# Second layer of a two-layer graph network on one Trainium2 core: table products of 26 candidates with the penalty rows inside them, and twelve of 40 edge columns by TensorE in place of ten

## The reference: what is computed

```python
x = _layernorm(x + _L0_gnn_ref(x, src, dst, edge_attr_3, edge_attr_10, edge_weight, W1, W2))
x = _layernorm(x + _L1_gnn_ref(x, attn_w, src, dst))
...
def _L1_gnn_ref(h, attn_w, src, dst):
    s_src = h @ attn_w[:d]
    s_dst = h @ attn_w[d:]
    e = s_src[src] + s_dst[dst]
    e = jnp.where(e >= 0, e, LEAKY_SLOPE * e)
    m = jax.ops.segment_max(e, dst, num_segments=N)
    ex = jnp.exp(e - m[dst])
    denom = jax.ops.segment_sum(ex, dst, num_segments=N)
    alpha = ex / denom[dst]
    return jax.ops.segment_sum(h[src] * alpha[:, None], dst, num_segments=N)
```

## Time and profile before

| | |
|---|---|
| time, median of 3 runs | 5710.63 us (5705.38 to 5717.29) |
| span of the profiled execution | 4918.3 us |
| time of a run beside that span | 792.3 us |
| TensorE busy (matmul) | 3925.7 us, 80% of the span |
| GpSimd busy | 3457.8 us, 70% |
| VectorE busy | 3366.4 us, 68% |
| ScalarE busy | 1665.0 us, 34% |

### The profile page before, as it was taken

How to read it: one execution, slowest core, us unless ns; L and a number is a source line. 1 busy time by engine, 2 the same in 40 slices (tenths; PEclk the granted TensorE clock), 3 DMA queues, 4 the chain that set the end, 5 groups by cost and what they waited for, 6 DMA issues and landing times. The chain is left out here.

```text
span 4918.3 us, 76839 instructions
## 1 busy us (share of the span) xinstructions
PE 3925.7 (80%) x22447; PEld 2433.8 (49%) x22447; DVE 3366.4 (68%) x5756; ACT 1665.0 (34%) x3062; POOL 3457.8 (70%) x3515
## 2 busy tenths in 40 slices
PE   0007999999999999999999600899999999999950
PEld 0004555545544555555555300677777777777740
DVE  4517999999999999999999540455555555555532
ACT  3005666666665666666666300001010100001000
POOL 5777777777666666666663177677777777777766
PEclk9999999999999999999999855899999999999975
DMA  9412222222222222222221000222222222222211
GB/s 327 135 35 50 46 44 45 44 44 46 47 44 43 43 43 43 43 43 43 49 46 30 21 11 14 55 48 46 45 48 48 45 47 49 49 49 49 49 27 25
DMA packets 266830, 253.17 MB, mean 51 GB/s; under 512 B 182298, under 2 KB 237026, under 8 KB 263867
## 3 DMA queue, kind: packets, MB, share of 16 engines
q1 hardware_dynamic: 157118, 174.83, 13.1%
q0 software_dynamic: 109024, 72.30, 9.5%
q10 hardware_dynamic: 462, 4.00, 0.3%
HBM read 160.55 MB, written 90.34 MB: 51 GB/s over the span
## 5 line engine op out<-in xcount | busy, mean ns | idle before, releaser
L626 POOL DMA_INDIRECT edge<-xp_d,idx x1440 | 1437.2, 998 | 634.6 <-issue 358.5
L1231 POOL DMA_INDIRECT gxb<-tab_d,idxb x1200 | 1290.6, 1075 | 376.6 <-issue 324.9
L890 DVE TENSOR_TENSOR prod<-G_ps,hid 128x1000 f32<-128x1000 f32 x1200 | 1385.5, 1192 | 67.0 <-ACT hid L685 39.1
L782 PE MATMUL G_ps<-FT,wst 64*128 64x500 f32 x4800 | 937.9, 434 | 38.2 <-DVE prod L890 38.2
L1266 PE MATMUL G_ps<-tb,hot 125*126 125x500 f32 (+1 forms) x3200 | 675.5, 364 | 333.0 <-DVE hotk L1288 299.7
L792 PE MATMUL R_ps<-prod,red 128*32 128x500 f32 x4800 | 769.4, 601 | 0.0
L1266 PEld LDWEIGHTS G_ps<-tb,hot 125*126 125x126 f32 x3200 | 546.3, 192 | 449.1 <-issue 349.8
L782 PEld LDWEIGHTS G_ps<-FT,wst 64*128 64x128 f32 x4800 | 421.6, 187 | 467.1 <-issue 263.9
L766 PE MATMUL T_ps<-ident,HL 125*128 125x125 f32 x3200 | 519.0, 285 | 129.1 <-DVE HL L880 128.4
L679 ACT ACTIVATE FT<-T_ps 128x500 fp32r<-128x500 f32 x800 | 470.0, 590 | 204.5 <-PE T_ps L766 192.6
L766 PEld LDWEIGHTS T_ps<-ident,HL 125*128 125x128 f32 x3200 | 332.7, 141 | 411.6 <-issue 274.4
(11 more groups left out here) (247 smaller groups left out, 4636.9 us busy)
## 6 DMA issues: line engine op xcount, KB each, us to landing
xd_d<-zeros SPq DMA_DIRECT2D x16, 1562.5 KB, 29.0
y_d<-zrb SPq DMA_DIRECT2D x40, 595.0 KB
edge<-xp_d,idx POOLq DMA_INDIRECT x1440
xv<-xd_d SPq DMA_DIRECT2D x40, 560.0 KB
y_d<-zr SPq DMA_DIRECT2D x40, 560.0 KB
edge<-sel_d SPq DMA_DIRECT2D x40, 546.9 KB
gxb<-tab_d,idxb POOLq DMA_INDIRECT x1200
em<-in_edge_attr SPq DMA_DIRECT2D x40, 175.0 KB
```

The source lines that it names most:

```text
L626: nc.gpsimd.indirect_dma_start(out=edge_c[:, i, 8:8 + DIM], out_offset=None, in_=xp_d, in_offset=bass.IndirectOffsetOnAxis(col, 0)).then_i ...
L782: last = Tn.matmul(G_ps[(k * 3 + i) % 2][:, a * 512:a * 512 + GW], wst[a * 64:(a + 1) * 64, (2 * i + l) * 128:(2 * i + l + 1) * 128], FT[k ...
L890: V.tensor_tensor(prod[k][i][:, :].rearrange("p (a e) -> p a e", a=2), gv, hid[k][:, :].rearrange("p (a e) -> p a e", a=1).broadcast_to([1 ...
L1231: nc.gpsimd.indirect_dma_start(out=gx[h][:, c * T1:(c + 1) * T1], out_offset=None, in_=tab_d, in_offset=bass.IndirectOffsetOnAxis(idx[h][: ...
```

## The change

A group of candidates is 26 wide in place of 25 (`KL`), so 104 nodes stand on a partition and 121 partitions hold them all; seven partitions of 128 are free. These take the penalty: `tb[0]` holds on them -2^100 for each candidate whose place is not the partition's (the 4 x 7 free rows hold at least 26 places), and the node rows of SP hold there the place of each edge within its group (`sel_d[1]`) where the other 121 hold its partition and group. The column vectors `iot` are shifted on these seven partitions to match. So the same four one-hots per chunk, now on 128 partitions, select the data and the penalty, and `far`, `hotk` and their two products per column go. The features are split 17 and 16 (442 and 416 wide). `XC` is 12, so GpSimd gathers 28 columns per chunk. The table is no longer made piece by piece from `x1e`: its layout of 104 nodes per partition is read back from `tab_d` into `xt1` by three DMAs of SP, and ScalarE and VectorE make the high and low parts from that, four copies and four subtractions after the fourth piece. The first block makes two more index patterns and the shifted `iot`.

```diff
-    XC = 10
+    XC = 12
...
-    KL = 25
+    KL = 26
+    PR = 121
+    NR = NG4 * KL
+    KR = PG - PR
...
-    FU = 20
-    GS = KL * (DIM + 1) + 1
+    FU = 17
+    GS = KL * (DIM + 1)
...
+                    nc.gpsimd.iota(own_i[:, :], [[0, 1]], base=0, channel_multiplier=1).then_inc(S("a_iota"), 1)
+                    nc.gpsimd.iota(kio_i[:, :], [[1, KL]], base=0, channel_multiplier=0).then_inc(S("a_iota"), 1)
...
+                    step(V.tensor_scalar(krow[:, :], krow[:, :], float(PR) - 0.5, -float(PR), ALU.is_ge, ALU.mult))
+                    for g in range(NG4):
+                        step(V.scalar_tensor_tensor(iot[:, g:g + 1], krow[:, :], g + 1.0, iot[:, g:g + 1], ALU.mult, ALU.add))
...
                     step(V.memset(sd[:, :], 0.0))
-                    for l in range(2):
-                        step(V.memset(tb[l][:, :].rearrange("p (g w) -> p g w", w=GS)[:, :, GS - 1].bitcast(f32), 0.0))
-                    step(V.tensor_scalar(far[:, :].rearrange("p (f k) -> p f k", k=KL),
-                                         ident[0:KL, 0:KL].rearrange("p (f k) -> p f k", f=1).broadcast_to([KL, FU, KL]), -1.0, FAR, ALU.add, ALU.mult))
...
+                    V.memset(xt1[:, :], 0.0).then_inc(S("c_tb0"), 1)
+                    V.memset(tb[1][:, :].bitcast(f32), 0.0).then_inc(S("c_tb0"), 1)
+                    for g in range(NG4):
+                        V.tensor_scalar(by_feature(tb[0], g, PG), kio[:, :].rearrange("p (f k) -> p f k", f=1).broadcast_to([PG, DIM + 1, KL]),
+                                        iot[:, g:g + 1], -FAR, ALU.not_equal, ALU.mult).then_inc(S("c_tb0"), 1)
...
+                    act.wait_ge(S("c_tb0"), 2 + NG4)
+                    act.wait_ge(S("c_tab"), 80)
+                    for g in range(NG4):
+                        nc.scalar.activation(by_feature(tb[0], g, PR), by_node(g), ACT.Copy).then_inc(S("c_hi"), 1)
...
+                    sp.wait_ge(S("c_tb0"), 1)
+                    rows = tab_d[0:(PR - 1) * NR, :].rearrange("(p k) f -> p (k f)", k=NR)
+                    for r in (slice(0, PS), slice(PS, PR - 1)):
+                        sp.dma_start(xt1[r, :], rows[r]).then_inc(S("c_tab"), 16)
...
                         for l in range(2):
                             for g in range(NG4):
                                 for (f0, f1, w), ps in zip(FUS, slot):
-                                    nc.tensor.matmul(ps[0:PE2, 0:w], hot[h][:, g * XP + j * P:g * XP + j * P + PE2],
-                                                     tb[l][:, g * GS + f0 * KL:g * GS + f0 * KL + w], start=(l == 0 and g == 0), stop=False)
-                        for (f0, f1, w), ps in zip(FUS, slot):
-                            last = nc.tensor.matmul(ps[0:PE2, 0:w], hotk[h][:, j * P:j * P + PE2], far[:, 0:w], start=False, stop=True)
+                                    last = nc.tensor.matmul(ps[0:PE2, 0:w], hot[h][:, g * XP + j * P:g * XP + j * P + PE2],
+                                                            tb[l][:, g * GS + f0 * KL:g * GS + f0 * KL + w],
+                                                            start=(l == 0 and g == 0), stop=(l == 1 and g == NG4 - 1))
...
-                        V.tensor_scalar(hotk[h][:, 0:XP], nodek[h], iot[0:KL, 0:1], None, ALU.is_equal).then_inc(S("d_hot"), 1)
```

More of the change, by code:

```diff
@@ L55, in gnn_resnorm_kernel @@
     C121 = 1.5 ** 0.5
-    XC = 10
+    XC = 12
     CG = C - XC
     NG4 = 4
-    KL = 25
+    KL = 26
+    PR = 121
+    NR = NG4 * KL
+    KR = PG - PR
+    assert PR * NR >= N and (PR - 1) * NR < N and NG4 * KR >= KL
     XP = XC * P
-    FU = 20
-    GS = KL * (DIM + 1) + 1
+    FU = 17
+    GS = KL * (DIM + 1)
     PE2 = P + 1
@@ L190, in gnn_resnorm_kernel @@
             SELB = NSEL // 4
-            iot_i = sbt("iot_i", [P, NG4], i32)
+            iot_i = sbt("iot_i", [PG, NG4], i32)
+            own_i = sbt("own_i", [PG, 1], i32)
+            krow = sbt("krow", [PG, 1])
+            kio_i = sbt("kio_i", [PG, KL], i32)
             ssel, psel, ksel, gsel = [sq[:, a * NSEL:(a + 1) * NSEL] for a in range(4)]
@@ L1029, in gnn_resnorm_kernel @@
         both = ExitStack()
-        tb = [both.enter_context(nc.sbuf_tensor(f"tb{l}", [P, NG4 * GS], f32r)) for l in range(2)]
-        far = both.enter_context(nc.sbuf_tensor("far", [KL, FU * KL], f32r))
-        assert NG4 * KL == NP and KP == KL and NPIECE == NG4
+        tb = [both.enter_context(nc.sbuf_tensor(f"tb{l}", [PG, NG4 * GS], f32r)) for l in range(2)]
         with ExitStack() as st:
@@ L1043, in gnn_resnorm_kernel, with by_feature, by_node @@
             sd = sbt("sd", [PG, NP])
-            def by_feature(ap, i):
-                return ap[:, i * GS:i * GS + KL * (DIM + 1)].rearrange("p (f k) -> p f k", k=KL)
-            def by_node(i):
-                return piece_of(x1e, i, DIM + 1).rearrange("p k f -> p f k")
+            xt1 = sbt("xt1", [PR, NR * (DIM + 1)])
+            def by_feature(ap, g, rows):
+                return ap[0:rows, g * GS:(g + 1) * GS].rearrange("p (f k) -> p f k", k=KL)
+            def by_node(g):
+                return xt1[:, g * GS:(g + 1) * GS].rearrange("p (k f) -> p f k", f=DIM + 1)
             with nc.Block() as block:
@@ L1123, in _ @@
                         nc.scalar.activation(stt[:, 2 * NP + i * KP:2 * NP + (i + 1) * KP], stt[:, NP + i * KP:NP + (i + 1) * KP], ACT.Sqrt).then_inc(S("ln_std"), 1)
-                        act.wait_ge(S("c_x1e"), i + 1)
-                        nc.scalar.activation(by_feature(tb[0], i), by_node(i), ACT.Copy).then_inc(S("c_hi"), 1)
+                    act.wait_ge(S("c_tb0"), 2 + NG4)
+                    act.wait_ge(S("c_tab"), 80)
+                    for g in range(NG4):
+                        nc.scalar.activation(by_feature(tb[0], g, PR), by_node(g), ACT.Copy).then_inc(S("c_hi"), 1)
                 @block.sync
@@ L1148, in gnn_resnorm_kernel @@
             gx = [sbt(f"gxb_{h}", [PG, C * T1]) for h in range(2)]
-            hot = [sbt(f"hot_{h}", [P, NG4 * XP + 2], f32r) for h in range(2)]
-            hotk = [sbt(f"hotk_{h}", [KL, XP + 2], f32r) for h in range(2)]
-            nodes = [edge[0:P, h * XP:(h + 1) * XP] for h in range(2)]
-            nodek = [edge[0:KL, (2 + h) * XP:(3 + h) * XP] for h in range(2)]
-            FUS = ((0, FU, FU * KL), (FU, T1, (T1 - FU) * KL + 1))
+            hot = [sbt(f"hot_{h}", [PG, NG4 * XP + 2], f32r) for h in range(2)]
+            nodes = [edge[:, h * XP:(h + 1) * XP] for h in range(2)]
+            FUS = ((0, FU, FU * KL), (FU, T1, (T1 - FU) * KL))
             SLOTS = [(G_ps[0][:, 0:512], G_ps[0][:, 512:1024]), (G_ps[1][:, 0:512], G_ps[1][:, 512:1024]),
@@ L1179, in load_nodes @@
                         if not isinstance(ch, int):
-                            sp.wait_ge(S("d_hot"), ch * 5 - 5)
+                            sp.wait_ge(S("d_hot"), ch * NG4 - NG4)
                             sp.sem_inc(S("go"), 1)
-                        for a, t in ((0, nodes[h]), (1, nodek[h])):
-                            rows = sel_d[a].rearrange("i p -> (i p)")[bass.ds(ch * XP, XP)].rearrange("(a f) -> a f", a=1).broadcast_to([t.shape[0], XP])
-                            if a == 0:
-                                by_rows(sp, t, rows, S(f"d_nd{h}"))
-                            else:
-                                sp.dma_start(t, rows).then_inc(S(f"d_nd{h}"), 16)
+                        for a, r0, r1 in ((0, 0, PS), (0, PS, PR), (1, PR, PG)):
+                            rows = sel_d[a].rearrange("i p -> (i p)")[bass.ds(ch * XP, XP)].rearrange("(a f) -> a f", a=1).broadcast_to([r1 - r0, XP])
+                            sp.dma_start(nodes[h][r0:r1, :], rows).then_inc(S(f"d_nd{h}"), 16)
                     def load(ch, h, t):
```

32 lines of the change are left out of this document (17 added, 15 removed).

## The result

The changed kernel took 5749.99 us (median of 4, 5737.16 to 5756.64), the kernel before 5708.01 beside it (5697.20 to 5717.29): ratio 1.0071, 95% interval 1.0055 to 1.0087. The forecast was 5693 us, 0.3% faster, with a range of 5650 to 5722; the kernel is 0.7% slower, outside the range.

The account below looks back on a forecast made before the run. Gathers were taken to bound the second layer's loop at 41.4 us per chunk, the new bound being 40.9. Loop -22.4 and +4.6 between the layers made -17.8 us, from 5710.6 to 5693 us; range 5650 to 5722.

Parts of the forecast that it names:

- 792.3 us beside the span: Whole run: time of 5710.6 us less the profiled span of 4918.3, left unchanged in the sum.
- Period 40.9 us: Second layer's loop, per chunk: 39.8 us plus 1.1 for slow columns, in place of 41.4; loop 22.4 us shorter.
- 14.7 us and eight columns: Second layer's chunk: VectorE's absence of 14.7 us plus eight columns of 3.14 gives 39.8 us, above the gathers' 39.0.
- Column of 3.14 us: TensorE, second layer's loop: eight new pairs of 0.392 us with no pauses left, 3.14 us a column.
- rivals 2 and 3: Second-layer columns: 2, border pause stays, 3.34 us, 5714 us (0.20); 3, all pauses stay, 3.56 us, 5785 us (0.11).
- rival 4: TensorE streams at the full rate, column 2.86 us, gathers bind at 39.0 us: 5617 us (chance 0.04).
- Stall of 2.1 us: TensorE, once per chunk: VectorE's absence of 14.7 us less the 12.6 us covered by four columns.
- 0.72 x 1.5: TensorE after the stall: 13 in 18 chance of a slow column costing 1.5 us, 1.1 us per chunk.
- Rival 1: TensorE's clock stays up, no slow columns, period 39.8 us: 5651 us (chance 0.17).
- The gathers' 39.0 us: GpSimd, second layer's loop: 28 gathers of 1.25 us plus 4.0 per chunk, under the 39.8 us bound.
- +4.6 between the layers: VectorE's clears and fills ahead of the carried row add 4.6 us to the path, bounds +2 and +8.
- Hidden work: Table through DRAM, preparing work before the first layer, and larger node rows: all covered, costing nothing.

Follow-up runs that it names:

- experiment 1: Both kernels rerun unchanged: the kernel before 5713.35 us, ratio 0.9996, span 5711.1; the changed kernel 5753.44 us, ratio 1.0085.
- new_table_10: Changed kernel with ten columns by TensorE in place of twelve, the new table alone: 5713.39 us, ratio 1.0002 to the kernel before.
- base_again: The kernel before, run again unchanged for a second trace: 5713.35 us, ratio 0.9996.
- experiment 3: Changed kernel with the next one-hot made after four picks: 5729.79 us with twelve columns, 5704.91 us with ten.
- experiment 7: Changed kernel making only 4 of a chunk's 28 gathers after the first two chunks, leaving work out: 5624.51 us, ratio 0.9695 to the kernel before.
- Experiment 4: Changed kernel with six fills of the new table moved below the addition of the carried row: 5742.62 us, ratio 1.0068 to the kernel before.
- experiment 5: Changed kernel without the waits that pace GpSimd's gathers by TensorE's columns: 6451.49 us, ratio 1.1311 to the kernel before.
- narrow_products: Changed kernel with 14 of a column's 16 products streaming only 128 columns, leaving work out: 5771.57 us, ratio 1.0110 to the kernel before.
- few_gathers: Changed kernel making only 4 of a chunk's 28 gathers after the first two chunks: 5624.51 us, ratio 0.9695 to the kernel before.
- after_third: Changed kernel run once more unchanged, beside the best version: 5756.54 us, ratio 1.0094 to the kernel before.

## Why the prediction was wrong, point by point

- **The step that failed** is in the sum: "The time of a run holds 792.3 us beside the span (5710.6 less 4918.3), which I leave as it is". They lie inside the span, 627 and 138 of them in the two loops (experiment 1). The section ahead of the prediction made the same step, where it says that they lie outside what the trace shows. I had taken a trace that was 14% shorter than the time for the shape of the run and the missing time for a constant. With it fell **"Period 40.9 us"**: the executions that are timed have a pause of 4.0 us per chunk in the changed kernel.
- *Why the pause turns a gain into a loss.* Before, the gathers bind; TensorE has slack, its pause goes into that, and only GpSimd's waits in it, 3.5 us per chunk in new_table_10 and 4.1 in base_again, add to its gathers' 41 to 41.5 (44.9 measured, mean over 39 periods). After, TensorE and VectorE bind, as forecast, and 4.0 us stand in their cycle with no slack beside them. It is not a fixed cost on top: experiment 3 took 3.9 us out of the same cycle and the pause grew by 3.8. The forecast's period of 14.7 us and eight columns is a cycle with no slack left. The new bound itself was forecast, and without the pause it measures what was forecast (41.06 in experiment 7 against 40.9); what it was exposed to was not.
- *Column of 3.14 us*: right (3.135), and nothing at the border, so rivals 2 and 3 fall, though the time came out on rival 3's side. The excess over full rate stayed, so rival 4 falls. By the Trainium skill's rule on the issue gap, as cited in the prediction, it would be 2.90; the trace decides against it for this pair. That section gives the rule for an isolated product and says that at large widths it over-counts a stream of products with their weight loads; here the stream takes 392 ns per pair and the rule gives 362, so it under-counts.
- *Stall of 2.1 us and "0.72 x 1.5" for the slow column*: 2.49 and 1.43 (33 of 38 chunks were slow, 13 in 18 assumed). Together 0.7 us per chunk too little, 27 us over the loop: by itself this would have made 5693 into 5720, just inside the range. Rival 1, the clock that stays up, falls.
- *The gathers' 39.0 us below the bound, and no wait of VectorE for them*: right. GpSimd stands, as forecast, but for 3.4 us ahead of a chunk's first gather in place of 1 to 2, and 3.0 more in the pause (means, each beyond the usual 0.30).
- *+4.6 between the layers*: 7.7, inside its bounds (+2 and +8). The clears came as forecast (2.92 us each), but the four fills take 4.02 us in place of the 2.16 that the one-hots' rate gave, and 1.4 us of idle time stand ahead of the two clears. GpSimd's first DMA, which the upper bound would have held up, comes 17.5 us after the last edge product, as before (17.6). Experiment 4 shows that the 7.7 were avoidable.
- *Hidden work*: no sign of a cost. From the stored row between the layers to the first table product are 295.3 us in the changed kernel and 298.8 in the kernel before, so the table's way through DRAM is covered; the first edge product starts at 415.6 to 424.8 us in the traces with the new preparing block and at 416.3 in the second trace of the kernel before.

What stays open: why gathers beside TensorE's products slow the latter down and delay their counts. Whether it is their packets, their instructions or something else of theirs was not taken apart. Half the bytes gathered and 96 more instructions on ScalarE left it as it was; the clock and the load of the DMA engines do not explain it (1.00 and 0.08 in the pause shown above). Nothing points to a refill of TensorE's instructions either: from 3925 to 5500 us, 34 chunks with their pauses, the DMA queues of the changed kernel are these two (packets, MB, share of 16 engines), and no instruction queue is among them:

```profile
q1 hardware_dynamic: 27000, 52.03, 11.0%
q0 software_dynamic: 30976, 16.42, 8.2%
```

(The Trainium skill, "Runtime: NRT & Kernel Launch", section "Instruction fetch mechanics", has a sequencer refill its instructions in blocks by a DMA queue of its own, and stall where a branch leaves its window. By it the pause could have been such a refill; the rows show none.) Open too is why the first execution had no pauses, and the 627 us in the first layer's loop, on which nothing was tried.

## What to carry to other kernels

Compare a trace's span with the run's time before anything is taken from it; where they differ by more than runs do, the trace isn't of the run, and a balance of engines worked out from it says nothing of slack. Moving work from the engine that binds to one that is nearly as full exposes every pause that slack had swallowed. And when a split between two engines changes, the waits that pace one by the other belong to the change: here `c % 3`, right for 30 gathers to ten columns, was left standing for 28 to twelve.

## What the runs showed of the hardware that I had not expected

- With GpSimd's gathers at full rate (one per 1.25 us) beside TensorE's columns, TensorE fell to a product per 0.7 to 2.8 us for as long as they went on (some 22 us in experiment 5), and a finished column was counted 26 us late. It ended 2.4 and 4.8 us after the last gather in the two chunks shown (3910.94 to 3913.36; 4458.73 to 4463.49). Every trace with all its gathers shows pauses or late counts but one, the first of the kernel before.
- In narrow_products the granted clock stayed at its lower level for the whole loop of 1805 us, TensorE being busy 97% of it, so that less work took longer: a column 3.70 us in place of 3.14.
- The same kernel took 5705 to 5713 us on three chips and 5805 on a fourth, where the first layer's loop was longer too (last edge product at 3488 in few_gathers, 3428 in after_third). Ratios held: 0.9817 and 0.9816 for the same kernel.
